# Fourth layer of a graph network: messages summed over edges before they are reduced, in four quadrants of TensorE

## The reference

```python
h = relu(edge_scalars @ (fc_w1 / sqrt(8))) * sqrt(2)            # E x 256
w = (h @ (fc_w2 / sqrt(256))).reshape(E, 4, 8, 8)               # E x 256
x = node_features[edge_src]; s1 = x[:, :8]; v1 = x[:, 8:].reshape(E, 8, 3)
s2 = edge_sh[:, 0]; v2 = edge_sh[:, 1:4]
out_s = A * (einsum('eu,euw->ew', s1*s2, w[:,0]) + INV_SQRT3 * einsum('eui,ei,euw->ew', v1, v2, w[:,1]))
out_v = B * (einsum('eu,euw,ei->ewi', s1, w[:,2], v2) + einsum('eui,euw->ewi', v1*s2, w[:,3]))
node_out = segment_sum(concat([out_s, out_v]), edge_dst)
```

## Time and profile before

| What | Value |
| --- | --- |
| Median of 3 runs | 14886.34 us (14883.05 to 14889.52) |
| The profiled execution | 14891.23 us, its span 14889.4 us |
| Share of the span: PE, DVE, ACT, POOL | 79%, 87%, 53%, 67% |
| TensorE's granted clock, mean over the span | 0.888 |

### The profile page before, as it was taken

How to read it: one execution, slowest core, us unless ns; L and a number is a source line. 1 busy time by engine, 2 the same in 40 slices (tenths; PEclk the granted TensorE clock), 3 DMA queues, 4 the chain that set the end, 5 groups by cost and what they waited for, 6 DMA issues and landing times. The chain is left out here.

```text
span 14889.4 us, 427370 instructions
## 1 busy us (share of the span) xinstructions
PE 11746.5 (79%) x109342; PEld 9054.7 (61%) x109342; DVE 12928.2 (87%) x30182; ACT 7888.3 (53%) x23572; POOL 9996.3 (67%) x10549
## 2 busy tenths in 40 slices
PE   1555555555548999999999999979788888888888
PEld 1444444444446666666666666667666666666666
DVE  5777777777768999999999999977799999999997
ACT  0555555555536666666666666638344444444443
POOL 4777777777756666666666666638577777777775
PEclk8666666666669999999999999979899999999999
DMA  3555555555542222222222222238211111111111
GB/s 94 84 87 87 86 87 86 87 87 87 87 67 38 36 36 36 36 36 36 36 36 36 36 36 36 36 116 293 57 24 24 24 24 24 24 24 24 24 24 23
DMA packets 2705891, 840.21 MB, mean 56 GB/s; under 512 B 2232498, under 2 KB 2650073, under 8 KB 2704124
## 3 DMA queue, kind: packets, MB, share of 16 engines
q1 hardware_dynamic: 2212179, 616.76, 20.7%
q0 software_dynamic: 312320, 178.52, 9.2%
q10 hardware_dynamic: 181250, 43.25, 1.3%
HBM read 610.22 MB, written 226.58 MB: 56 GB/s over the span
## 5 line engine op out<-in xcount | busy, mean ns | idle before, releaser
L1352 POOL DMA_INDIRECT w_rows<-table,w_idx x9375 | 8929.7, 952 | 4086.9 <-issue 2387.3
L1583 PE MATMUL w_p_w<-w_w,w_ht 128*128 128x256 f32 x12500 | 3007.2, 388 | 125.1 <-DVE w_prodv L1527 124.5
L1335 PE MATMUL w_p_deg<-w_hot_lo,w_hot_row 128*128 128x196 bf16 x6250 | 1797.5, 336 | 1573.4 <-DVE w_hot_lo L1280 1535.0
L1583 PEld LDWEIGHTS w_p_w<-w_w,w_ht 128*128 128x128 f32 x12500 | 2273.1, 190 | 673.5 <-issue 299.4
L1147 ACT ACTIVATE w_dist<-row_iota,w_negrel 128x32 f32<-128x32 f32 x9375 | 2182.6, 315 | 300.1 <-issue 272.2
L1554 ACT ACTIVATE w_ht<-w_p_h 128x512 f32<-128x512 f32 x1875 | 851.2, 526 | 2489.6 <-PE w_p_h L1574 2489.6
L1793 DVE TENSOR_TENSOR w_prod<-w_p_xe,w_he 128x512 f32<-128x512 f32 x3125 | 2137.5, 684 | 4.3 <-PE w_p_xe L1936 4.3
L1309 ACT CAST w_counts<-w_p_count 128x784 uint8<-128x784 f32 x1875 | 1247.2, 706 | 1453.3 <-PE w_p_count L1336 1435.9
L1335 PEld LDWEIGHTS w_p_deg<-w_hot_lo,w_hot_row 128*128 128x128 bf16 x6250 | 829.9, 133 | 1698.1 <-issue 1607.8
L1336 PE MATMUL w_p_count<-w_hot_lo,w_hot_row 128*128 128x196 bf16 x6250 | 1808.6, 336 | 0.0
L1959 PE MATMUL w_p_sgt<-w_prod,w_wc 128*32 128x128 f32 x25000 | 1331.6, 284 | 85.9 <-ACT w_sgt L1872 65.7
(11 more groups left out here) (211 smaller groups left out, 20273.9 us busy)
## 6 DMA issues: line engine op xcount, KB each, us to landing
counts<-w_counts SPq DMA_DIRECT2D x1250, 122.5 KB
d_small<-counts SPq DMA_DIRECT2D x388, 392.0 KB
w_rows<-table,w_idx POOLq DMA_INDIRECT x9375
w_rel_row<-rel_row SPq DMA_DIRECT2D x625, 120.0 KB
w_edge<-e SPq DMA_DIRECT2D x625, 80.0 KB
w_idx<-src SPq DMA_DIRECT2D x1875, 2.5 KB
w_negrel<-negrel SPq DMA_DIRECT2D x1875, 2.5 KB
w_nodes<-split SPq DMA_DIRECT2D x1875, 2.0 KB
```

Source lines behind the costliest of these rows:

```text
L1335: nc.tensor.matmul(p_deg[:], hot_row[s2][:, b, :], hot_lo[s2][:, b, :], start=False, stop=False, skip_group_check=True)
L1352: pool.indirect_dma_start(out=rows[:, t, :], out_offset=None, in_=table[0:N, :], in_offset=bass.IndirectOffsetOnAxis(ap=idx[:, t:t + 1], a ...
L1583: last = nc.tensor.matmul(p_w[(g.base * len(BANKS) + bank) % WBANKS][:, (t - t0) * 256:(t - t0 + 1) * 256], ht[g.slot(UNROLL)][:, k, t * P ...
```

## The change

The message is no longer formed on each edge. The products go, unreduced, into a tile `mix` of 344 columns per edge and tile: 128 for the scalars (8 sums of 16) and 216 for the vectors (24 sums of 9). The one-hot, now the stationary operand of 32 columns, sums these columns over the edges on PE: tiles 0 to 3 go to four quadrants of the array and of PSUM's partitions, and tile 4 is cut into four slices of 86 columns, one for each quadrant. DVE then reduces the 128 x 344 sums in PSUM to 128 x 32 (`fold`), and one matmul with four stacked identities (`stack_d`, now 128 rows) adds the quadrants and turns them into the 32 x 32 that `add_window` adds.

On PE, `sum_edges` of the group three steps old stands between bank 0 and bank 1 of the next group's weights, and `sum_quarters` after bank 2. On DVE the fold stands between bank 0 and bank 1; `add_window` now follows the reduction of `prodt`, and the ninth terms come last and give `msg_ready`. `prods`, `prodv`, `msg` and the two message reductions are gone; `mix` has two buffers. The diff, cut to its core:

```diff
+class QuarterSums:
+    def one_hot(self, act, g, negrel):
...
+    def sum_edges(self, pe, g, tile, rest):
+        hot, matmul = self.hot[g.slot(UNROLL)], self.nc.tensor.matmul
+        done(pe, self.hot_ready, g)
+        free(pe, self.acc_added, g, 1)
+        pe.nop(nofuse=True)
+        for q in range(4):
+            matmul(self.p_mix[WIN * q:WIN * (q + 1), :], hot[:, q, :], tile(q), start=True, stop=False, skip_group_check=True)
+        for q in range(4):
+            columns, part = rest(q)
+            last = matmul(self.p_mix[WIN * q:WIN * (q + 1), columns], hot[:, 4, :], part, start=False, stop=True, skip_group_check=True)
+        last.then_inc(self.mix_ready, 1)
+    def sum_quarters(self, pe, g):
+        done(pe, self.held_ready, g)
+        self.nc.tensor.matmul(self.p_acc, self.held[g.slot(2)][:], self.a["stack_d"][:], start=True, stop=True).then_inc(self.acc_ready, 1)
+    def add_window(self, dve, g):
+        base = dve.value_load(self.a["base_sb"][0:1, bass.ds(g.times(1), 1)], min_val=0, max_val=N - 1)
+        done(dve, self.acc_ready, g)
+        free(dve, self.acc_added, g, 1)
+        nodes = self.a["acc_t"][0:self.width, bass.ds(base, WIN)]
+        self.nc.vector.tensor_add(nodes, nodes, self.p_acc).then_inc(self.acc_added, 1)
...
-        p_acc = ps("p_acc", [2 * D, WIN])
+        p_sum = ps("p_sum", [P, 512])
+        w = QuarterSums(nc, a, 3, sb, p_sum[:, 0:MIX], p_sum[0:D, MIX:MIX + WIN], D)
-        msg = [sb(f"msg{s}", [P, T, D]) for s in range(UNROLL)]
+        mix = [sb(f"mix{s}", [P, T, MIX]) for s in range(2)]
...
+            def products(g, b):
+                gs, to = rows[g.slot(UNROLL)], mix[g.slot(2)]
...
+                vec.tensor_mul(to[:, t0:t1, 0:SCALAR].rearrange("p t (w u) -> p t w u", u=16),
+                               pw[:, :, 0:128].rearrange("p t (w u) -> p t w u", u=16), spread(x16[:, t0:t1, :], [P, n, 8, 16], 2))
...
+                    last = vec.tensor_mul(to[:, t, SCALAR:MIX].rearrange("p (k w u) -> p k w u", k=3, u=9)[:, :, :, 0:8],
...
+            def fold(g):
+                held = w.held[g.slot(2)]
+                done(dve, w.mix_ready, g)
+                free(dve, w.acc_ready, g, 2)
+                vec.tensor_reduce(held[:, 0:8], w.p_mix[:, 0:SCALAR].rearrange("p (w u) -> p w u", u=16), AX.X, ALU.add)
+                vec.tensor_reduce(held[:, 8:32].rearrange("p (w k) -> p k w", k=3),
+                                  w.p_mix[:, SCALAR:MIX].rearrange("p (k w u) -> p k w u", k=3, u=9), AX.X, ALU.add).then_inc(w.held_ready, 1)
...
+                if g := at(2):
+                    factors(g)
+                    products(g, 0)
+                if g := at(3):
+                    fold(g)
+                if g := at(2):
+                    products(g, 1)
+                    products(g, 2)
                     dve.wait_ge(w_used, g.times(len(BANKS), len(BANKS)))
                     vec.tensor_reduce(rt[:], prodt[:].rearrange("p t (w u) -> p t w u", u=8), AX.X, ALU.add).then_inc(red_ready, 1)
-                    vec.tensor_reduce(msg[sm][:, :, 0:8], prods[:].rearrange("p t (w u) -> p t w u", u=16), AX.X, ALU.add)
-                if g := at(5):
+                if g := at(3):
                     w.add_window(dve, g)
                 if g := at(2):
-                    vec.tensor_reduce(msg[g.slot(UNROLL)][:, :, 8:32].rearrange("p t (w k) -> p t k w", k=3),
-                                      prodv[:].rearrange("p (t k) (w u) -> p t k w u", k=3, u=9), AX.X, ALU.add).then_inc(msg_ready, 1)
+                    done(dve, red_ready, g)
+                    vec.tensor_mul(mix[g.slot(2)][:, :, SCALAR:MIX].rearrange("p t (k w u) -> p t w k u", k=3, u=9)[:, :, :, :, 8],
+                                   spread(rt[:], [P, T, 8, 3], 3), spread(harm[g.slot(UNROLL)][:, :, 1:4], [P, T, 8, 3], 2)).then_inc(msg_ready, 1)
...
                 if g := at(2):
-                    for bank, (t0, t1) in enumerate(BANKS):
...
-                if g := at(4):
-                    w.sum_window(pe, g, msg[g.slot(UNROLL)], msg_ready)
+                    weigh(g, 0)
+                if g := at(3):
+                    done(pe, msg_ready, g)
+                    w.sum_edges(pe, g, lambda t: mix[g.slot(2)][:, t, :], lambda q: (slice(SLICE * q, SLICE * (q + 1)), mix[g.slot(2)][:, 4, SLICE * q:SLICE * (q + 1)]))
+                if g := at(2):
+                    weigh(g, 1)
+                    weigh(g, 2)
+                if g := at(3):
+                    w.sum_quarters(pe, g)
```

More of the change, by code:

```diff
@@ L174, in _ @@
                     pool.wait_ge(consts, k)
-            for i in range(SPLIT):
+            for i in range(P // D):
                 pool.affine_select(out=a["stack_d"][:], in_=a["stack_d"][:], compare_op=ALU.not_equal, fill=1.0, base=-D * i,
@@ L1168, in add_window, with __init__ @@
         self.nc.vector.tensor_add(nodes, nodes, self.p_accs[g.slot(self.accs)]).then_inc(self.acc_added, 1)
+class QuarterSums:
+    def __init__(self, nc, a, layer, sb, p_mix, p_acc, width):
+        self.nc, self.a, self.width, sem = nc, a, width, a["sems"][layer]
+        self.p_mix, self.p_acc = p_mix, p_acc
+        self.dist = [sb(f"dist{s}", [P, T, WIN]) for s in range(2)]
+        self.hot = [sb(f"hot{s}", [P, T, WIN]) for s in range(UNROLL)]
+        self.held = [sb(f"held{s}", [P, width]) for s in range(2)]
+        self.dist_ready, self.hot_ready, self.mix_ready, self.held_ready, self.acc_ready, self.acc_added = (
+            sem(n) for n in ("dist_ready", "hot_ready", "mix_ready", "held_ready", "acc_ready", "acc_added"))
+    def one_hot(self, act, g, negrel):
+        dist = self.dist[g.slot(2)]
+        free(act, self.hot_ready, g, 2)
+        for t in range(T):
+            last = self.nc.scalar.activation(dist[:, t, :], self.a["row_iota"][:, 0:WIN], ACT.Abs, bias=negrel[:, t:t + 1])
+        last.then_inc(self.dist_ready, 1)
+        done(act, self.dist_ready, g)
+        free(act, self.mix_ready, g, UNROLL)
+        self.nc.scalar.activation(self.hot[g.slot(UNROLL)][:], dist[:], ACT.Relu, scale=-1.0, bias=1.0).then_inc(self.hot_ready, 1)
+    def sum_edges(self, pe, g, tile, rest):
[18 more added lines that the diff above has]
+        self.nc.vector.tensor_add(nodes, nodes, self.p_acc).then_inc(self.acc_added, 1)
@@ L1431, in window_pass_3 @@
     BANKS, WBANKS = ((0, 2), (2, 4), (4, T)), 4
+    SCALAR, VECTOR = 8 * 16, 3 * 8 * 9
+    MIX = SCALAR + VECTOR
     with ExitStack() as ctx:
@@ L1438, in window_pass_3 @@
         p_w = [ps(f"p_w{s}", [P, 512]) for s in range(WBANKS)]
-        w = WindowPass(nc, a, 3, sb, [p_acc[D * s:D * (s + 1), :] for s in range(2)], hots=UNROLL)
+        w = QuarterSums(nc, a, 3, sb, p_sum[:, 0:MIX], p_sum[0:D, MIX:MIX + WIN], D)
         idx = [sb(f"idx{s}", [P, T], I32) for s in range(UNROLL)]
@@ L1451, in window_pass_3 @@
         dots = sb("dots", [P, T, MUL3, 3])
-        prods = sb("prods", [P, T, 128])
         prodt = sb("prodt", [P, T, 64])
-        prodv = sb("prodv", [P, T * 3, 8 * 9])
         rt = sb("rt", [P, T, 8])
@@ L1458, in window_pass_3 @@
         gathered = [sem(f"gathered{s}") for s in range(UNROLL)]
-        dots_ready, x_ready, w_used, red_ready, vout_ready, msg_ready, h_mm, ht_ready, w_mm, weights_in, weights_ready = (
-            sem(n) for n in ("dots_ready", "x_ready", "w_used", "red_ready", "vout_ready", "msg_ready", "h_mm", "ht_ready",
+        dots_ready, x_ready, w_used, red_ready, msg_ready, h_mm, ht_ready, w_mm, weights_in, weights_ready = (
+            sem(n) for n in ("dots_ready", "x_ready", "w_used", "red_ready", "msg_ready", "h_mm", "ht_ready",
                              "w_mm", "weights_in", "weights_ready"))
@@ L1503, in _, with factors @@
             load_weights_3(nc, w2_in, w2).then_inc(weights_ready, 1)
+            def factors(g):
+                gs, sh = rows[g.slot(UNROLL)], harm[g.slot(UNROLL)]
+                arrived(dve, loaded, g, LOADS)
+                arrived(dve, gathered, g, GATHERED)
+                free(dve, msg_ready, g, 1)
+                v8 = gs[:, :, 8:32].rearrange("p t (u k) -> p t u k", k=3)
+                vec.tensor_mul(dots[:], v8, spread(sh[:, :, 1:4], [P, T, 8, 3], 2)).then_inc(dots_ready, 1)
+                vec.tensor_mul(x16[:, :, 0:8], gs[:, :, 0:8], sh[:, :, 0:1].to_broadcast([P, T, 8]))
+                vec.tensor_mul(sv[:].rearrange("p t k u -> p t u k"), v8, sh[:, :, 0:1].unsqueeze(3).to_broadcast([P, T, 8, 3]))
+                done(dve, dots_ready, g)
+                vec.tensor_reduce(x16[:, :, 8:16], dots[:], AX.X, ALU.add).then_inc(x_ready, 1)
+                done(dve, x_ready, g)
+                free(dve, w.mix_ready, g, 2)
@@ new lines, in products @@
+            def products(g, b):
+                gs, to = rows[g.slot(UNROLL)], mix[g.slot(2)]
+                t0, t1 = BANKS[b]
+                n, pw = t1 - t0, p_w[(g.base * len(BANKS) + b) % WBANKS][:, 0:(t1 - t0) * 256].rearrange("p (t c) -> p t c", c=256)
```

(26 more changed lines are left out.)

4 lines of the change are left out of this document (removed).

## The result

The changed kernel takes 14660.69 us (median of 4 runs, 14659.61 to 14665.89) beside 14885.82 us before (median of 4 runs): a ratio of 0.9849, 95% interval 0.9832 to 0.9866. Forecast were 14671 us. The profiled execution has a span of 14664.2 us, 225.2 less than before.

The account below looks back on a forecast made before the run. DVE bounds the fourth layer at 6.765 us a step; afterwards PE would at 6.42. The gain of 0.345 x 624 = 215 us takes 14891.2 to 14676, and 4.9 lower gives 14671 us; range 14570 to 14800.

Parts of the forecast that it names:

- PE's new sum: PE's work in one step of the fourth layer, switches of array shape included: 6.44 us, or 6.39 without a 0.05 wait.
- the edge sums with the way out: PE's narrow matmuls over the edges in four quadrants, 0.75 us, plus 0.10 us for the switch out.
- the folded sum with the way out: PE's one 32x32 matmul of the folded sums in each step: 0.03 us plus 0.13, after 0.10 us of switch in.
- The upper bound of 0.94 for the streams alone: PE's edge-sum passes at the pace of the second layer's L1959: 0.94 us instead of 0.75, PE's sum then 6.6.
- The rule weighed against it: Skill page's 3.07 times for four tiles of 512 columns: 2.9 us in series become 0.94, PE's sum 6.6 us.
- The fold: DVE's two new reductions out of PSUM, 128 and 216 elements: 0.27 and 0.36 us, 0.5 together less overlap.
- The register load: DVE's load of the window's place, ahead of addition L1168: 0.95 us from reduction start to addition instead of 0.41.
- the chain: Last multiplication on DVE, PE's edge sums and bank 1, DVE's banks 1 and 2, reduction, addition, last multiplication: 6.21 us.
- The rival that it binds: The chain through PE and DVE sets the step, 6.5 to 6.7 us; at 6.6 the time is 14783; chance 0.20.
- DVE's wait for bank 1: In each step DVE waits some 0.5 us for PE's bank 1.
- POOL's gap between groups: POOL's pause between one group's gathers and the next, a sign to look for: nearer 0.4 than 0.8 us.
- The 5.8 us that I summed: DVE's new sum for one step of the fourth layer, fold and exposed register load included: 5.8 us.

## Why the prediction was right, point by point

- **DVE bounds the kernel before; the bound moves to PE.** Right. PE at 1000 of 1000 us after, and the run with more work on DVE costs nothing.
- **PE's new sum, 6.39 to 6.44 us.** Measured 6.41. Its terms: the edge sums with the way out 0.85, measured 0.87; the folded sum with the way out 0.16 (0.03 + 0.13), measured 0.19; the rest, with the two ways in, 5.38 to 5.43, measured 5.35. So small errors in both directions cancel, none above 0.08 us. The upper bound of 0.94 for the streams alone was not needed: from the first record of 344 columns to the first of 86 it is 0.60 us, two passes of 0.29 and little else. In every group the first four of these matmuls start within 0.02 us of each other (the sign named was 0.03). The excess of 0.03 us a pass at 128 columns in the earlier trace rows did not grow with the columns: it is 0.01 a pass here.
- **The rule weighed against it.** The page "TensorE: Matmul & The Clock Gate" of the Trainium skill (Part 3, measured speedup vs the span model) gives 3.07 times for four tiles. Its row is for tiles of 32 rows; the tiles here are of 32 columns, for which it lists three tiles, at 2.38 times. Here eight passes of 0.29 us take 0.60 us side by side, 3.9 times, and the measurement decides.
- **The fold, 0.27 and 0.36 us.** Measured means of 281 and 373 ns, 0.01 us each above the line through the reductions of the earlier trace rows; so reading PSUM cost little here.
- **The register load comes into the open.** Right: 0.91 us from the reduction's start to the addition's in the timeline above, forecast 0.95. Its price in the chain is 0.50 us (forecast 0.95 - 0.41 = 0.54).
- **The chain has 0.2 us to spare.** Measured 0.24. The rival that it binds was near: 0.24 us more in the chain, half of what the register load costs there, would have brought it level with PE.
- **DVE's wait for bank 1, 0.5 us.** 321.9 / 593 = 0.54.
- **POOL's gap between groups nearer 0.4 than 0.8 us.** Right: 0.5 us is the longest in the view of waits.
- **DVE's busy share of about 85%.** Too high: 80%. The 5.8 us that I summed run from start to start and hold waits on its own results and the gap of 0.4 us; the busy time is 0.797 x 6.41 = 5.1. Nothing hung on it.
- **The total.** 215 us were forecast; 219.5 came from the layer's steps, and 5.7 from outside them, mostly the end of the layer, which the prediction did not count.

## What to carry to other kernels

Before an engine is relieved, add up what the next engines need in one step, switches and waits included: of the almost 1 us by which the forecast's sum for DVE fell (6.765 to 5.8) only 0.35 became time, since PE's sum stood at 6.4 us and POOL's at 6.3. Sums over edges of data that are ten times wider (344 columns in place of 32) took PE 0.87 us when narrow matmuls ran in four quadrants, and 2.15 us a step more when they ran in one. Try narrow stretches side by side: gathering two of them into one saved PE 0.33 us a step here, though POOL's gathers let only 0.117 of it become time.

## What was not expected of the hardware

That the register load comes into the open was forecast; what it costs was not what the idle time of 0.41 us shows, but 0.50 us of the chain. On DVE's sequencer the loads of two steps stand so, in the changed kernel (L1213, behind the reduction) and with the load moved ahead (behind the fold):

```profile
L1213 DVEq TENSOR_LOAD <-base_sb x2: 303/310/316, 13005.6 to 13012.0; - x2
...
L1213 DVEq TENSOR_LOAD <-base_sb x2: 302/307/312, 13003.4 to 13009.8; - x2
...
13003.77 0.37 DVE L1591 TENSOR_REDUCE w_held<-w_p_sum 128x24 f32<-128x216 f32 x1
```

In the changed kernel the reduction L1602 waits on a semaphore; it starts at 13011.91 us, and the load behind it at 13012.0, so the load did not run ahead of that wait. Moved ahead, the load starts at 13003.4, 0.4 us before the fold's second reduction (13003.77) that stands before it in the program. Of POOL's gathers I had taken 1.252 us each from the rows before; issued without a break between groups, with the edge sums last, they come every 1.258 us.
